# Routing the first four tiles of a mixture of experts ahead of the other twelve, in an eight-block transformer kernel on one Trainium2 core

## Chip, cores and metric

The kernel runs on one core of a Trainium2 chip. The metric is the device time of one execution in microseconds (us); less is better. Engines: PE (matrix products), DVE (VectorE), ACT (ScalarE), POOL (GpSimd), SP (which issues the loads).

## The reference

The input is x of shape (2, 1024, 128), fp32: 2048 tokens, D = 128. Eight residual blocks follow each other, each on the layer-normed x: a window attention, a mixture of experts, a causal attention, the same mixture again, a cope attention, a six-layer local stack, a linear attention, and the local stack again. The change touches the mixture:

```python
logits = xt @ gate_w.T                      # (2048, 8)
scores = softmax(logits); top_vals, idx = top_k(scores, 2)
xs = xt[:, None, :] * weights[:, :, None]   # weights: the scores of the chosen
for e in range(8):
    mask = (idx == e)
    h  = silu(xs @ w1[e].T + b1[e])         # 128 -> 128
    x2 = h @ w2[e].T + b2[e]
    x3 = xs @ w3[e].T + b3[e]
    y  = y + sum(x2 * x3 * mask)
z = silu(xt @ sw1.T) * (xt @ sw2.T) @ sw3.T # shared expert, 256 wide
x = x + y + z
```

## The kernel before

X (2048 tokens as NT = 16 tiles of 128 tokens on the partitions) stays in SBUF through all blocks. A block is a stage: each engine has its own program, written out by hand in the order in which it is to run (`pe`, `act`, `dve`, `pool`), and waits on semaphores for the others; a barrier (`fence`) ends the stage. `mixture` is run twice, with the tags `f_` and `g_`, on the same weights, which were loaded long before; no DMA is issued in it.

All eight experts are computed for every token, with the score as scale and a 0/1 mask of the two best. In the beginning the 16 tiles are normed in four groups of four: DVE measures (lines 202 to 209), POOL takes the power (213), DVE applies (222), PE transposes (238), ACT copies the result to XNT (245), PE multiplies the four tiles by the gate (603). Then DVE copies the four groups' gate outputs (716) and does the softmax for all 16 tiles at once (656 to 664), with ACT's Exp between (621). PE waits at line 605 for the copies of all groups before its first large product.

The loop over the tiles follows. For tile i:
- PE `up(i)` (572, 576): eight w1, eight w3 and the shared expert's products, banks 0 to 4 of PSUM; the last waits for `zadd_out`.
- DVE `up(i)` (689) scales w1's products by the score and adds b1; ACT does Silu on them (633); PE turns them (563), ACT copies (628), PE `down(i)` (584).
- ACT does Silu of the shared half (637), DVE multiplies by the other half (`gated`, 695), PE turns it (590), ACT copies (649), PE `shared_down` (596), DVE adds to X (722).
- ACT scales w3's products to x3 (644). POOL adds b3 (738) and multiplies by the mask (740).
- DVE `down(i)` adds b2 (703) and multiplies by x3 (707). POOL adds the eight experts in three steps (745), and to X (748).

The order on DVE is: z add of tile i-1, `up(i)`, `gated(i)`, at i = 0 `choose()`, `down(i-1)`. The order on POOL is: b3 and mask of tile i, then the tree of tile i-1; after tile 15 one more tree ends the stage. `choose()` (671 to 681) makes the mask for all 16 tiles with five instructions of 1024 elements and one of 128: two comparisons of each score with each other, a product with a table that settles ties, a sum, a reduction, and "fewer than 1.5 rivals". At tile 0 ACT waits for that mask before it scales x3 (line 641).

Of the kernel before, what the change touches and what calls it, by code (L numbers as in the profile page):

```python
# [9 lines left out]
ALU = mybir.AluOpType  # L10
# [43 lines left out]
def build(nc, t, out):  # L54
    ctx = ExitStack()
    with ctx:
# [477 lines left out]
        def mixture(tag):  # L534
            with ExitStack() as own:
# [12 lines left out]

                def xt(i):
                    return XNT[:, A_WIN + i * P:A_WIN + (i + 1) * P]

                def pe():
# [41 lines left out]
                            m = te.matmul(PS[:, 4, I_SH:I_SH + D], sT[:, j * P:(j + 1) * P], sw3[:, j, :], start=(j == 0), stop=(j == 1))  # L596
                        m.then_inc(z_mm)

                    for g in range(NG):
                        norm_turn(g, xn4[:, g % 2, :, :])  # L600
                        te.wait_ge(xT_out, g + 1)
                        for j in range(4):
                            m = te.matmul(PS[:, 1 + g, j * E_N:(j + 1) * E_N], xt(4 * g + j), gate[:, :], start=True, stop=True)
                        m.then_inc(gate_mm)
                    te.wait_ge(gate_out, NG)
                    for i in range(NT + 1):
                        if i:
                            turn(i - 1)
                            shared_down(i - 1)
                        if i < NT:  # L610
                            up(i)
                        if i:
                            down(i - 1)
                        if i < NT:
                            shared_turn(i)

                def act():
                    for g in range(NG):
                        norm_copy(g, kept_T(g))
                    ac.wait_ge(scores_out, 1)  # L620
                    ac.activation(sc[:, :, :], sc[:, :, :], ACT.Exp).then_inc(sc_exp)
                    for i in range(NT + 1):
                        if i:
                            for n, bank in ((0, 6), (1, 5)):
                                ac.wait_ge(h_turn, 2 * (i - 1) + n + 1)
                                if i >= 2:
                                    ac.wait_ge(y_mm, 2 * (i - 2) + n + 1)
                                ac.copy(hT[:, 4 * n:4 * n + 4, :].rearrange("p a b -> p (a b)"), PS[:, bank, :]).then_inc(hT_out)
                        if i < NT:
                            for n in range(2):  # L630
                                h = hin[:, i % 2, 4 * n:4 * n + 4, :]
                                ac.wait_ge(hin_out, 2 * i + n + 1)
                                ac.activation(h, h, ACT.Silu).then_inc(silu_out)
# [12 lines left out]
                            ac.wait_ge(sg_turn, i + 1)  # L646
                            if i >= 1:
                                ac.wait_ge(z_mm, i)
                            ac.copy(sT[:, :], PS[:, 4, 0:I_SH]).then_inc(sT_out)

                def dve():
                    all3, four = [P, NT, E_N], [P, NT, E_N, E_N]

                    def scores():
                        V.wait()
                        V.step(ve.tensor_reduce(r1[:, :], sc[:, :, :], AX, ALU.max))
                        V.wait()
                        ve.tensor_tensor(sc[:, :, :], sc[:, :, :], over(r1[:, :], 2, all3), ALU.subtract).then_inc(scores_out)
                        ve.wait_ge(sc_exp, 1)
                        V.step(ve.tensor_reduce(r1[:, :], sc[:, :, :], AX, ALU.add))  # L660
                        V.wait()
                        V.step(ve.reciprocal(r1[:, :], r1[:, :]))
                        V.wait()
                        V.step(ve.tensor_tensor(sc[:, :, :], sc[:, :, :], over(r1[:, :], 2, all3), ALU.mult))
                        V.wait()

                    def choose():
                        gt4 = gt[:, :, :].rearrange("p t (a b) -> p t a b", a=E_N)
                        eq4 = eq[:, :, :].rearrange("p t (a b) -> p t a b", a=E_N)
                        rival, own_s = over(sc[:, :, :], 2, four), over(sc[:, :, :], 3, four)  # L670
# [3 lines left out]
                        V.step(ve.tensor_tensor(eq[:, :, :], eq[:, :, :],  # L674
                                                over(lower[:, :, :].rearrange("p a b -> p (a b)"), 1, [P, NT, E_N * E_N]), ALU.mult))
                        V.wait()
                        V.step(ve.tensor_tensor(gt[:, :, :], gt[:, :, :], eq[:, :, :], ALU.add))
                        V.wait()
                        V.step(ve.tensor_reduce(mask[:, :, :], gt4, AX, ALU.add))
                        V.wait()  # L680
                        ve.tensor_scalar(mask[:, :, :], mask[:, :, :], 1.5, None, ALU.is_lt).then_inc(mask_out)

                    def up(i):
                        if i >= 2:
# [24 lines left out]
                    norm_stats(0, X)  # L709
                    for g in range(NG):  # L710
                        if g < NG - 1:
                            norm_stats(g + 1, X)
                        norm_apply(g, X, xn4[:, g % 2, :, :])
                    for g in range(NG):
                        ve.wait_ge(gate_mm, g + 1)
                        ve.tensor_copy(sc[:, 4 * g:4 * g + 4, :], PS[:, 1 + g, 0:4 * E_N].rearrange("p (j e) -> p j e", j=4)).then_inc(gate_out)
                    ve.wait_ge(gate_out, NG)
                    scores()
                    for i in range(NT + 1):
                        if i:  # L720
                            ve.wait_ge(z_mm, i)
                            ve.tensor_tensor(X[:, i - 1, :], PS[:, 4, I_SH:I_SH + D], X[:, i - 1, :], ALU.add).then_inc(zadd_out)
                        if i < NT:
                            up(i)
                            gated(i)
                        if i == 0:
                            choose()
                        if i:
                            down(i - 1)

                def pool():
                    for g in range(NG):
                        norm_root(g)
                    for i in range(NT + 1):
                        if i < NT:
                            x = x3[:, i % 2, :, :]
                            gp.wait_ge(x3_out, 2 * i + 2)
                            G.step(gp.tensor_tensor(x, x, b3[:, :, :], ALU.add))
                            G.wait()
                            gp.tensor_tensor(x, x, over(mask[:, i, :], 2, [P, E_N, D]), ALU.mult).then_inc(x3m_out)  # L740
                        if i:
# [1284 lines left out]
```

## Time and profile before

| | |
|---|---|
| median of 3 runs | 4230.68 us (4227.46 to 4234.22) |
| profiled execution | 4232.35 us, span 4230.3 us, mean granted TensorE clock 0.947 |
| PE busy | 3803.1 us, 90% of the span |
| DVE busy | 3017.7 us, 71% |
| POOL busy | 2675.5 us, 63% |
| ACT busy | 2586.9 us, 61% |
| first mixture, first norm to the next stage's first norm | 169.78 to 343.36 us |
| second mixture, the same | 415.74 to 589.19 us |

The profile is one execution. Times in it are counted from the span's start; "busy" leaves out waits. The two mixtures together are 347 us of 4230, the two local stacks some 3,200. Matrix products in fp32 are done in several passes, so a product of the code shows as more than one instruction. "idle before <- releaser" says how long the engine stood still before an instruction and what released it. The duration of a DVE or POOL instruction includes time in which it is issued but held up.

### The profile page before, as it was taken

The numbers are of one execution on the slowest core, as the hardware profiler recorded it, in microseconds if no ns is written. First come the engines' busy times: TensorE is split into PE (matmuls) and PEld (weight loads), VectorE is DVE, ScalarE is ACT, GpSimd is POOL, SyncE is SP. The second block draws the span as 40 slices with busy tenths as digits, with TensorE's granted clock in tenths as the row PEclk, the third lists the DMA queues.
The fourth block names the chain that finished last, engine by engine and source line by source line (L and its number), as shares of the span: only waits on it lengthen the run. The fifth ranks groups of instructions, "written<-read, shape, count | busy, mean of one in ns | idle before, by whom it ended". The sixth has DMA issues, their size and how long they took to land. (4 is left out here: it accounts for less than half of the span.)

```text
span 4230.3 us, 158783 instructions
## 1 busy us (share of the span) xinstructions
PE 3803.1 (90%) x66896; PEld 2661.8 (63%) x66896; DVE 3017.7 (71%) x6190; ACT 2586.9 (61%) x4965; POOL 2675.5 (63%) x2263
## 2 busy tenths in 40 slices
PE   7896863999999999999999568999999999999996
PEld 5564542666766666666666435676666666676664
DVE  6675657777777777877778257777877777777773
ACT  4463531667666676766676325666667676766764
POOL 2192663776767676767667237776767667676762
PEclk9898885999999999999999759999999999999998
DMA  3000000333333333333233102333333233332222
GB/s 100 1 1 1 1 1 0 98 79 79 83 75 89 82 80 80 80 80 91 65 94 80 34 0 70 85 77 91 78 80 95 66 92 79 78 90 71 70 65 56
DMA packets 303234, 276.83 MB, mean 65 GB/s; under 512 B 158136, under 2 KB 201664, under 8 KB 302528
## 3 DMA queue, kind: packets, MB, share of 16 engines
q1 hardware_dynamic: 302528, 266.68, 24.8%
q8 instruction: 533, 8.73, 0.9%
q14 instruction: 173, 1.42, 0.1%
HBM read 51.58 MB, written 1.05 MB: 12 GB/s over the span
## 5 line engine op out<-in xcount | busy, mean ns | idle before, releaser
L1433 PE MATMUL PS<-l_wqkv,XNT 128*128 128x512 f32 x768 | 386.0, 625 | 0.6 <-issue 0.5
L1427 PE MATMUL PS<-l_wqkv,XNT 128*128 128x512 f32 x768 | 381.1, 618 | 2.2 <-issue 1.1
L1420 PE MATMUL PS<-l_wqkv,XNT 128*128 128x512 f32 x768 | 366.7, 600 | 6.4 <-DVE l_UQ L1702 2.7
L1575 ACT ACTIVATE m_sq<-PS 128x512 f32<-128x512 f32 x384 | 226.1, 596 | 198.8 <-PE PS L1427 162.0
L1575 ACT ACTIVATE l_sq<-PS 128x512 f32<-128x512 f32 x384 | 226.2, 596 | 194.6 <-PE PS L1427 159.9
L1841 POOL TENSOR_TENSOR l_Pm<-l_Pm,l_rs 128x1024 f32<-128x1024 f32 x96 | 182.8, 1905 | 237.6 <-DVE l_rs L1712 237.6
L1841 POOL TENSOR_TENSOR m_Pm<-m_Pm,m_rs 128x1024 f32<-128x1024 f32 x96 | 182.8, 1904 | 235.8 <-DVE m_rs L1712 235.8
L1699 DVE TENSOR_TENSOR m_QR<-PS,l_rot 128x512 f32<-128x512 f32 x192 | 131.8, 687 | 165.2 <-ACT m_sq L1575 159.0
L1699 DVE TENSOR_TENSOR l_QR<-PS,l_rot 128x512 f32<-128x512 f32 x192 | 131.8, 687 | 163.4 <-ACT l_sq L1575 157.2
L1730 DVE TENSOR_TENSOR XN<-PS,XN 128x128 f32<-128x128 f32 x192 | 56.2, 293 | 269.3 <-PE PS L1479 269.3
L1836 POOL TENSOR_TENSOR m_QR<-m_QR,m_UQ 128x1024 f32<-128x1024 f32 x96 | 227.8, 2373 | 19.3 <-DVE m_UQ L1702 19.3
L1836 POOL TENSOR_TENSOR l_QR<-l_QR,l_UQ 128x1024 f32<-128x1024 f32 x96 | 227.7, 2372 | 19.0 <-DVE l_UQ L1702 19.0
L1836 POOL TENSOR_TENSOR l_KR<-l_KR,l_UK 128x1024 f32<-128x1024 f32 x96 | 226.9, 2363 | 0.2 <-DVE l_UK L1702 0.2
L1836 POOL TENSOR_TENSOR m_KR<-m_KR,m_UK 128x1024 f32<-128x1024 f32 x96 | 226.8, 2363 | 0.2 <-DVE m_UK L1702 0.2
L1717 DVE TENSOR_REDUCE m_sums<-m_sq 128x16 f32<-128x1024 f32 x192 | 219.1, 1183 | 0.0
L1717 DVE TENSOR_REDUCE l_sums<-l_sq 128x16 f32<-128x1024 f32 x192 | 219.1, 1183 | 0.0
L1449 PEld LDWEIGHTS PS<-l_V,l_pT 64*32 64x32 f32 x12288 | 132.7, 106 | 127.3 <-issue 69.9
L1449 PEld LDWEIGHTS PS<-m_V,m_pT 64*32 64x32 f32 x12288 | 131.2, 105 | 118.8 <-issue 81.3
L1433 PEld LDWEIGHTS PS<-l_wqkv,XNT 128*128 128x128 f32 x768 | 132.4, 192 | 114.0 <-issue 96.8
L1427 PEld LDWEIGHTS PS<-l_wqkv,XNT 128*128 128x128 f32 x768 | 130.7, 189 | 115.4 <-issue 95.9
L1449 PE MATMUL PS<-l_V,l_pT 64*32 64x64 f32 x12288 | 155.5, 228 | 48.0 <-DMA l_V<-l_Vt 31.5
L1420 PEld LDWEIGHTS PS<-l_wqkv,XNT 128*128 128x128 f32 x768 | 132.5, 193 | 102.2 <-issue 102.2
(373 smaller groups left out, 11170.7 us busy)
## 6 DMA issues: line engine op xcount, KB each, us to landing
l_V<-l_Vt SPq DMA_DIRECT2D x576, 128.0 KB
m_V<-m_Vt SPq DMA_DIRECT2D x576, 128.0 KB
l_V<-l_Vt SPq DMA_DIRECT2D x384, 64.0 KB
m_V<-m_Vt SPq DMA_DIRECT2D x384, 64.0 KB
l_wqkv<-l_wqkv_dram SPq DMA_DIRECT2D x144, 128.0 KB, 2.4
l_rot<-l_rot_dram SPq DMA_DIRECT2D x48, 256.0 KB, 3.9
l_wo<-l_wo_dram SPq DMA_DIRECT2D x24, 256.0 KB, 3.7
l_w<-l_w_dram SPq DMA_DIRECT2D x12, 341.0 KB
```

The source lines that it names most:

```text
L1420: te.matmul(PS[:, b, :], tile_T(n), weights(n, b * 512, (b + 1) * 512), start=True, stop=True).then_inc(q_pr)
L1427: te.matmul(PS[:, 2 + b, :], tile_T(n), weights(n, INNER + b * 512, INNER + (b + 1) * 512), start=True, stop=True).then_inc(k_pr)
L1433: m = te.matmul(PS[:, r, :], tile_T(n), wv, start=True, stop=True)
L1449: m = te.matmul(PS[LW * w:LW * (w + 1), 6 + r, c * LD:(c + 1) * LD], pT[64 * r:64 * r + 64, c, LW * w:LW * (w + 1)], V2[64 * r:64 * r + 64 ...
L1575: ac.activation(sq[:, c, b * 512:(b + 1) * 512], PS[:, 2 * c + b, :], ACT.Square).then_inc(sq_out)
L1699: ve.tensor_tensor(R[:, n % 2, heads, :], src, over(rot[:, par, 2 * c, i, :], 1, [P, 8, LD]), ALU.mult)
L1717: ve.tensor_reduce(sums2[:, c * LH:(c + 1) * LH, 0], sq[:, c, :].rearrange("p (h d) -> p h d", d=LD), AX, ALU.add).then_inc(ssr_out)
L1730: ve.tensor_tensor(Y[:, i, :], PS[:, 5, 0:D], Y[:, i, :], ALU.add).then_inc(y_add)
L1836: gp.tensor_tensor(R[:, n % 2, :, :], R[:, n % 2, :, :], U[:, :, :], ALU.add).then_inc((aq_out, ak_out)[c])
L1841: gp.tensor_tensor(pm, pm, over(rs[:, :], 2, [P, 16, 2 * LW]), ALU.mult).then_inc(pn_out)
```

## The change

The first group (tiles 0 to 3) is gated, its softmax done, and tile 0's products made, before the other groups are transposed and gated. The softmax of tiles 4 to 15 is done at i = 1 on DVE, its Exp on ACT behind tile 0; their masks are made in three slices of four tiles at i = 2, 3 and 4. ACT no longer waits for the mask; POOL does, before the mask's product of tiles 0, 4, 8 and 12. All gate outputs share PSUM bank 5, and the transposes alternate between banks 6 and 7. The tree of tile 15 and its add to X are moved from POOL to DVE.

```diff
+                FIRST, OTHERS = slice(0, 4), slice(4, NT)
...
-                    for g in range(NG):
-                        norm_turn(g, xn4[:, g % 2, :, :])
...
+                    def gates(g):
                         te.wait_ge(xT_out, g + 1)
...
+                        if g == 1:
+                            te.wait_ge(gate_out, 1)
+                        for i in range(4 * g, 4 * g + 4):
+                            m = te.matmul(PS[:, 5, i * E_N:(i + 1) * E_N], xt(i), gate[:, :], start=True, stop=True)
                         m.then_inc(gate_mm)
-                    te.wait_ge(gate_out, NG)
+
+                    rows_turn(0)
+                    gates(0)
+                    rows_turn(1)
+                    up(0)
+                    for g in range(2, NG):
+                        rows_turn(g)
+                        gates(g - 1)
+                    gates(NG - 1)
+                    te.wait_ge(gate_out, 2)
+                    te.wait_ge(xT_out, NG)
                     for i in range(NT + 1):
                         if i:
                             turn(i - 1)
                             shared_down(i - 1)
-                        if i < NT:
+                        if 0 < i < NT:
                             up(i)
...
                 def act():
...
+                    rows_copy(0)
+                    rows_copy(1)
+                    exponent(0, FIRST)
+                    rows_copy(2)
+                    rows_copy(3)
                     for i in range(NT + 1):
...
-                            if i == 0:
-                                ac.wait_ge(mask_out, 1)
...
+                        if i == 0:
+                            exponent(1, OTHERS)
...
                 def dve():
...
+                    def choose(tiles):
+                        n = tiles.stop - tiles.start
+                        four = [P, n, E_N, E_N]
+                        g_t, e_t, s_t = gt[:, tiles, :], eq[:, tiles, :], sc[:, tiles, :]
...
                         ve.tensor_tensor(gt4, rival, own_s, ALU.is_gt)
                         V.step(ve.tensor_tensor(eq4, rival, own_s, ALU.is_equal))
                         V.wait()
...
+                        V.step(ve.tensor_tensor(e_t, e_t, over(lower[:, :, :].rearrange("p a b -> p (a b)"), 1, [P, n, E_N * E_N]), ALU.mult))
                         V.wait()
...
+                        V.step(ve.tensor_tensor(g_t, g_t, e_t, ALU.add))
                         V.wait()
...
+                        V.step(ve.tensor_reduce(mask[:, tiles, :], gt4, AX, ALU.add))
                         V.wait()
...
+                        ve.tensor_scalar(mask[:, tiles, :], mask[:, tiles, :], 1.5, None, ALU.is_lt).then_inc(mask_out)
...
                         ve.tensor_tensor(y, y, x3[:, i % 2, :, :], ALU.mult).then_inc(y3_out)
...
+                        if i == NT - 1:
+                            ve.wait_ge(y3_out, NT)
+                            for n in (4, 2, 1):
+                                V.step(ve.tensor_tensor(y[:, 0:n, :], y[:, 0:n, :], y[:, n:2 * n, :], ALU.add))
+                                V.wait()
+                            ve.wait_ge(zadd_out, NT)
+                            V.step(ve.tensor_tensor(X[:, i, :], X[:, i, :], y[:, 0, :], ALU.add))
...
+                    stats(0)
+                    stats(1)
+                    apply(0)
+                    stats(2)
+                    apply(1)
+                    stats(3)
+                    ve.wait_ge(gate_mm, 1)
+                    take_gates(FIRST)
+                    shifted_scores(0, FIRST)
+                    apply(2)
+                    scores(0, FIRST)
+                    apply(3)
+                    up(0)
+                    gated(0)
+                    choose(FIRST)
+                    ve.wait_ge(gate_mm, NG)
+                    take_gates(OTHERS)
+                    shifted_scores(1, OTHERS)
+                    for i in range(1, NT + 1):
+                        ve.wait_ge(z_mm, i)
+                        ve.tensor_tensor(X[:, i - 1, :], PS[:, 4, I_SH:I_SH + D], X[:, i - 1, :], ALU.add).then_inc(zadd_out)
                         if i < NT:
                             up(i)
                             gated(i)
...
+                        down(i - 1)
+                        if i == 1:
+                            scores(1, OTHERS)
+                        if 2 <= i < 5:
+                            choose(slice(4 * i - 4, 4 * i))
 
                 def pool():
...
+                            if i % 4 == 0:
+                                gp.wait_ge(mask_out, 1 + i // 4)
                             gp.tensor_tensor(x, x, over(mask[:, i, :], 2, [P, E_N, D]), ALU.mult).then_inc(x3m_out)
-                        if i:
+                        if 0 < i < NT:
                             y = y8[:, (i - 1) % 2, :, :]
```

`rows_turn(g)` and `rows_copy(g)` are the norm's transposes and copies with the new banks; `take_gates`, `shifted_scores` and `scores` hold the instructions of lines 716 and 656 to 664 for a part of the tiles; `exponent` holds line 621.

## Rows read from the trace of the kernel before

**Rows 1.** Stage windows, tiles 1 to 15: length, busy us and instructions per engine, clock, DMA

```profile
206.00:331.00 125.00, 120.04 (x616) 80.00 (x614) 88.29 (x196) 75.52 (x210) 114.43 (x87) 0.99 0.00 1
```

**Rows 2.** Timeline, POOL: start, us, engine, line, operation, idle before and releaser

```profile
213.64 2.36 POOL L738 TENSOR_TENSOR f_x<-f_x,f_b 128x1024 f32<-128x1024 f32 x1 [5.61 <-ACT f_x L644]
216.08 2.76 POOL L740 TENSOR_TENSOR f_x<-f_x,f_mask 128x1024 f32<-128x1024 f32 x1
...
222.43 3.05 POOL L738 TENSOR_TENSOR f_x<-f_x,f_b 128x1024 f32<-128x1024 f32 x1 [0.49 <-ACT f_x L644]
225.55 1.90 POOL L740 TENSOR_TENSOR f_x<-f_x,f_mask 128x1024 f32<-128x1024 f32 x1
...
230.10 0.46 POOL L748 TENSOR_TENSOR X<-X,f_y 128x128 f32<-128x128 f32 x1
...
330.80 2.35 POOL L738 TENSOR_TENSOR f_x<-f_x,f_b 128x1024 f32<-128x1024 f32 x1
...
339.02 2.59 POOL L745 TENSOR_TENSOR f_y<-f_y 128x512 f32<-128x512 f32 x3
341.69 0.45 POOL L748 TENSOR_TENSOR X<-X,f_y 128x128 f32<-128x128 f32 x1
```

**Rows 3.** Timeline ahead of tile 0's x3, PE and ACT

```profile
177.26 1.09 PE L238 MATMUL PS<-ident,xn 128*128 128x128 f32 x4
...
188.19 5.19 PE L572 MATMUL PS<-f_w,XNT 128*128 128x512 f32 x8 [0.28 <-DVE f_sc L716]
...
189.14 1.28 ACT L633 ACT_TABLE_LOAD   x1
...
201.45 2.18 ACT L644 ACTIVATE f_x<-PS,f_sc 128x128 f32<-128x128 f32 x8 [6.79 <-DVE f_mask L681]
```

**Rows 4.** Timeline of tiles 1 to 3 and of the end, DVE, ACT and PE

```profile
213.69 3.39 DVE L707 TENSOR_TENSOR f_y<-f_y,f_x 128x1024 f32<-128x1024 f32 x1
...
217.21 2.14 DVE L689 SCALAR_TENSOR_TENSOR f_hin<-PS,f_sc,f_b 128x128 f32<-128x128 f32 x8
...
219.38 0.63 ACT L633 ACTIVATE f_hin<-f_hin 128x512 f32<-128x512 f32 x1 [0.40 <-DVE f_hin L689]
...
222.04 1.23 DVE L707 TENSOR_TENSOR f_y<-f_y,f_x 128x1024 f32<-128x1024 f32 x1
...
223.21 3.60 PE L572 MATMUL PS<-f_w,XNT 128*128 128x512 f32 x8
...
335.16 2.27 DVE L707 TENSOR_TENSOR f_y<-f_y,f_x 128x1024 f32<-128x1024 f32 x1 [2.99 <-POOL f_x L740]
```

**Rows 5.** DVE groups: one line's min/median/max ns; one group's busy us and mean ns

```profile
L1215 DVE TENSOR_TENSOR d_den<-d_dots x4: 224/224/1236, 2442.3 to 2501.6; 128x64 f32<-128x64 f32 x4
...
L995 DVE TENSOR_TENSOR c_gates<-c_gates 128x256 f32<-128x256 f32 x1 | 0.4, 424 | 0.0
```

**Rows 6.** Windows of one us, PE: length, busy us and instructions, granted clock, DMA

```profile
203.00:204.00 1.00, 0.06 (x1) 0.50 0.00 0
...
208.00:209.00 1.00, 1.00 (x3) 0.85 0.00 0
```

**Rows 7.** Timeline, ACT in the local stack: a table load and what follows

```profile
2013.88 1.28 ACT L1672 ACT_TABLE_LOAD   x1
2015.17 1.19 ACT L1575 ACTIVATE l_sq<-PS 128x512 f32<-128x512 f32 x2
```

**Rows 8.** Timeline, DVE and POOL in the linear attention

```profile
2500.20 1.26 POOL L1294 TENSOR_TENSOR d_an<-d_an,d_gain 128x512 f32<-128x512 f32 x1 [1.96 <-ACT d_an L1193]
2501.04 0.57 DVE L1214 TENSOR_TENSOR d_dots<-d_dots,d_turn 128x128 f32<-128x128 f32 x1
2501.54 1.26 POOL L1296 TENSOR_TENSOR d_an<-d_an,d_gain 128x512 f32<-128x512 f32 x1
2501.64 1.24 DVE L1215 TENSOR_TENSOR d_den<-d_dots 128x64 f32<-128x64 f32 x1
...
2502.92 1.27 DVE L1216 TENSOR_SCALAR d_den<-d_den 128x64 f32<-128x64 f32 x1
```

More of the change, by code:

```diff
@@ L597, in shared_down, with rows_turn @@
                         m.then_inc(z_mm)
-                    for g in range(NG):
-                        norm_turn(g, xn4[:, g % 2, :, :])
+                    def rows_turn(g):
+                        te.wait_ge(xn_out, g + 1)
+                        if g >= 2:
+                            te.wait_ge(xT_out, g - 1)
+                        for j in range(4):
+                            m = te.transpose(PS[:, 6 + g % 2, j * P:(j + 1) * P], xn4[:, g % 2, j, :], ident[:, :])
+                        m.then_inc(turn_mm)
+                    def gates(g):
                         te.wait_ge(xT_out, g + 1)
-                        for j in range(4):
-                            m = te.matmul(PS[:, 1 + g, j * E_N:(j + 1) * E_N], xt(4 * g + j), gate[:, :], start=True, stop=True)
+                        if g == 1:
+                            te.wait_ge(gate_out, 1)
+                        for i in range(4 * g, 4 * g + 4):
+                            m = te.matmul(PS[:, 5, i * E_N:(i + 1) * E_N], xt(i), gate[:, :], start=True, stop=True)
                         m.then_inc(gate_mm)
-                    te.wait_ge(gate_out, NG)
+                    rows_turn(0)
[8 more added lines that the diff above has]
+                    te.wait_ge(xT_out, NG)
                     for i in range(NT + 1):
@@ L617, in act, with rows_copy, exponent @@
                 def act():
[L618 to L621, printed above, removed]
+                    def rows_copy(g):
+                        ac.wait_ge(turn_mm, g + 1)
+                        ac.copy(kept_T(g), PS[:, 6 + g % 2, :]).then_inc(xT_out)
+                    def exponent(part, tiles):
+                        ac.wait_ge(scores_out, part + 1)
+                        ac.activation(sc[:, tiles, :], sc[:, tiles, :], ACT.Exp).then_inc(sc_exp)
+                    rows_copy(0)
[3 more added lines that the diff above has]
+                    rows_copy(3)
                     for i in range(NT + 1):
@@ L649, in act, with take_gates @@
                             ac.copy(sT[:, :], PS[:, 4, 0:I_SH]).then_inc(sT_out)
+                        if i == 0:
+                            exponent(1, OTHERS)
                 def dve():
-                    all3, four = [P, NT, E_N], [P, NT, E_N, E_N]
-                    def scores():
-                        V.wait()
-                        V.step(ve.tensor_reduce(r1[:, :], sc[:, :, :], AX, ALU.max))
+                    def take_gates(tiles):
+                        ve.tensor_copy(sc[:, tiles, :], PS[:, 5, tiles.start * E_N:tiles.stop * E_N].rearrange("p (t e) -> p t e", e=E_N)).then_inc(gate_out)
@@ new lines, in shifted_scores, with scores @@
+                    def shifted_scores(part, tiles):
+                        n = tiles.stop - tiles.start
+                        ve.wait_ge(gate_out, part + 1)
+                        V.step(ve.tensor_reduce(r1[:, tiles], sc[:, tiles, :], AX, ALU.max))
+                        V.wait()
+                        ve.tensor_tensor(sc[:, tiles, :], sc[:, tiles, :], over(r1[:, tiles], 2, [P, n, E_N]), ALU.subtract).then_inc(scores_out)
+                    def scores(part, tiles):
+                        n = tiles.stop - tiles.start
+                        ve.wait_ge(sc_exp, part + 1)
+                        V.step(ve.tensor_reduce(r1[:, tiles], sc[:, tiles, :], AX, ALU.add))
@@ L657, in scores @@
                         V.wait()
-                        ve.tensor_tensor(sc[:, :, :], sc[:, :, :], over(r1[:, :], 2, all3), ALU.subtract).then_inc(scores_out)
-                        ve.wait_ge(sc_exp, 1)
-                        V.step(ve.tensor_reduce(r1[:, :], sc[:, :, :], AX, ALU.add))
+                        V.step(ve.reciprocal(r1[:, tiles], r1[:, tiles]))
                         V.wait()
-                        V.step(ve.reciprocal(r1[:, :], r1[:, :]))
+                        V.step(ve.tensor_tensor(sc[:, tiles, :], sc[:, tiles, :], over(r1[:, tiles], 2, [P, n, E_N]), ALU.mult))
@@ L663, in scores @@
                         V.wait()
[L664 to L670, printed above, removed]
+                    def choose(tiles):
+                        n = tiles.stop - tiles.start
+                        four = [P, n, E_N, E_N]
+                        g_t, e_t, s_t = gt[:, tiles, :], eq[:, tiles, :], sc[:, tiles, :]
+                        gt4, eq4 = (a.rearrange("p t (a b) -> p t a b", a=E_N) for a in (g_t, e_t))
+                        rival, own_s = over(s_t, 2, four), over(s_t, 3, four)
@@ L673, in choose @@
                         V.wait()
-                        V.step(ve.tensor_tensor(eq[:, :, :], eq[:, :, :],
-                                                over(lower[:, :, :].rearrange("p a b -> p (a b)"), 1, [P, NT, E_N * E_N]), ALU.mult))
+                        V.step(ve.tensor_tensor(e_t, e_t, over(lower[:, :, :].rearrange("p a b -> p (a b)"), 1, [P, n, E_N * E_N]), ALU.mult))
                         V.wait()
-                        V.step(ve.tensor_tensor(gt[:, :, :], gt[:, :, :], eq[:, :, :], ALU.add))
+                        V.step(ve.tensor_tensor(g_t, g_t, e_t, ALU.add))
                         V.wait()
-                        V.step(ve.tensor_reduce(mask[:, :, :], gt4, AX, ALU.add))
+                        V.step(ve.tensor_reduce(mask[:, tiles, :], gt4, AX, ALU.add))
                         V.wait()
-                        ve.tensor_scalar(mask[:, :, :], mask[:, :, :], 1.5, None, ALU.is_lt).then_inc(mask_out)
+                        ve.tensor_scalar(mask[:, tiles, :], mask[:, tiles, :], 1.5, None, ALU.is_lt).then_inc(mask_out)
                     def up(i):
@@ L707, in down @@
                         ve.tensor_tensor(y, y, x3[:, i % 2, :, :], ALU.mult).then_inc(y3_out)
[L709 to L712, printed above, removed]
-                        norm_apply(g, X, xn4[:, g % 2, :, :])
-                    for g in range(NG):
-                        ve.wait_ge(gate_mm, g + 1)
-                        ve.tensor_copy(sc[:, 4 * g:4 * g + 4, :], PS[:, 1 + g, 0:4 * E_N].rearrange("p (j e) -> p j e", j=4)).then_inc(gate_out)
@@ L717, in dve @@
-                    ve.wait_ge(gate_out, NG)
-                    scores()
-                    for i in range(NT + 1):
-                        if i:
-                            ve.wait_ge(z_mm, i)
-                            ve.tensor_tensor(X[:, i - 1, :], PS[:, 4, I_SH:I_SH + D], X[:, i - 1, :], ALU.add).then_inc(zadd_out)
+                        if i == NT - 1:
[5 more added lines that the diff above has]
+                            V.step(ve.tensor_tensor(X[:, i, :], X[:, i, :], y[:, 0, :], ALU.add))
@@ new lines, in stats, with apply @@
+                    def stats(g):
+                        norm_stats(g, X)
+                    def apply(g):
+                        norm_apply(g, X, xn4[:, g % 2, :, :])
+                    stats(0)
[8 more added lines that the diff above has]
+                    apply(2)
@@ L725, in dve @@
                             gated(i)
[L726 to L729, printed above, removed]
+                        down(i - 1)
[3 more added lines that the diff above has]
+                            choose(slice(4 * i - 4, 4 * i))
                 def pool():
@@ L739, in pool @@
                             G.wait()
+                            if i % 4 == 0:
+                                gp.wait_ge(mask_out, 1 + i // 4)
                             gp.tensor_tensor(x, x, over(mask[:, i, :], 2, [P, E_N, D]), ALU.mult).then_inc(x3m_out)
-                        if i:
+                        if 0 < i < NT:
                             y = y8[:, (i - 1) % 2, :, :]
```

## The prediction

> **What bounds the kernel now.** I read the stretch of a mixture by windows first, because the change touches nothing else (it issues and moves no DMA, and SP's queue has no part in it): in the 125 us between tile 1's gating and the last tile, PE is busy 120.04 us, POOL 114.43 and DVE 88.29 [rows 1]. So two engines are nearly full and DVE looks free for a third of the time. Then POOL's timeline [rows 2]: its first bias add of a tile (line 738) for tile 1 starts at 213.64 us after 5.61 us of idleness, for tile 2 at 222.43 after 0.49, and the one of tile 15 at 330.80 with no idleness noted: 117.16 us for 14 tiles, 8.37 each. From tile 3 on POOL never waits; it has six instructions per tile (3.05, really 2.35 when nothing blocks it, then 1.90, three adds and 0.45; the last five run from 225.55 to 230.56). The stage ends with POOL's own last sum at 342.14. Before the loop the reader should see how long everything waits for routing [rows 3]: PE ends the second group's transposes at 178.35, but starts the big matmuls at 188.19, and ACT can scale x3 of tile 0 only at 201.45, after 6.79 us of waiting for the mask. The second mixture, read the same way, repeats all this to a few hundredths, so I work one out and double it.
>
> **What the start gains.** `up(0)` on PE needs only group 0's transposed rows, and in its new place it begins at 178.35 instead of 188.19, 9.8 us sooner. What then stands before POOL's tile 1? `up(0)` costs 5.19 for eight passes and some 0.9 for the last two, partly at the low clock [rows 3]: it ends near 183.8. ACT now has both remaining copies of rows queued ahead of tile 0's Silu, and they wait for PE: two sets of transposes (about 0.6 each at the full clock, 1.09 at the low one) and one set of gates (eight short passes, about 1 by estimate) stand behind `up(0)`, then a copy of 0.6: 186.6. Then the Silu table, 1.28 [rows 3], which was hidden before and no longer is, since the compiler puts it right ahead of the first Silu: 187.9. Two Silus, the shared Silu and x3 take 3.6 (from 219.38 to 222.43 is 3.05, plus one more Silu start of 0.5 [rows 4]): POOL gets tile 0 at about 191.5. DVE meanwhile gates at 189.8 and then chooses for four tiles: five instructions of 256 elements at 0.42 [rows 5] and a short one, 2.4 us with gaps instead of 6.4. Its last one is due at about 192.0 and probably lands behind POOL's 2.35; then it ends at 194.1. PE waits for the copy of the other gates behind that choice, so it resumes at 194.4, at the low clock (in 203 to 204 us, where it had 0.06 us of work, the granted clock was 0.50, and it was 0.85 only in 208 to 209, four us after the work came back [rows 6]): ten transposes of 0.27, shared_down 1.2 and ten passes of 0.43 to 0.44 (eight take 3.60 [rows 4]) end at 202.7, and x3 plus gaps 2.5 later: 205.2 against 213.64, that is -8.4. If the last short instruction is not caught, -9.9. I take **-9.0**.
>
> **Two more table loads.** The second Exp stands between two Silus, so ACT loads three tables where it loaded one. A load takes 1.28 us and the next instruction starts 0.01 us behind it (2013.88 plus 1.28 is 2015.16, next at 2015.17 [rows 7]). From 195.4 on ACT has load, Exp, two copies, load: ready at about 199.7, before tile 1's first Silu is due at about 200.5. Cover: PE's slow restart. Without it, it would cost up to 2.6. I count 0.
> The Trainium skill ("ScalarE: Activation LUTs", What ACT_TABLE_LOAD costs) gives about 2.66 us for every switch, a 1.38 us drain with the load, and asks to batch activations by set, which speaks against this change. The trace shows no such drain beside its load. By the page the sum would be some 2.3 us per mixture, 5 in all, higher.
>
> **What the other groups' choice costs.** This is the term that decides. The diff puts the softmax of tiles 4 to 15 at i=1 and a choice for four tiles at i=2, 3 and 4, each time on DVE behind `down`, in a place where POOL has just been given x3 and is busy for 7.5 us. Alone, a slice costs the 2.4 us above. But look at what a DVE instruction that reads two tensors from SBUF does beside POOL: line 707 takes 1.23 alone and 3.39 or 2.27 when a POOL instruction is running [rows 4]. In the linear attention the same is seen in a chain of small ones [rows 8]: line 1214 takes 0.57, and ends when POOL's 1.26 us instruction does; POOL's next starts, and line 1215 takes 1.24 (alone 0.22, [rows 5]); and then line 1216, a tensor_scalar, 1.27. So the two take turns by whole instructions, also across a semaphore gap. A slice has four two-input instructions and one tensor_scalar; each waits for one POOL instruction, so that DVE gets out only when POOL has finished all its six: from the start of line 738 that is 7.5 (POOL) + 1.2 (line 707) + 1.3 to 1.4 (what of the slice is not under POOL's) or about 10. From DVE's freedom to the next x3 at POOL is 5.4: z add 0.2, then 217.21 to 222.43 [rows 4]. One tile with a slice so lasts about **15.4** instead of 8.37. PE, queued behind zadd_out and sg_out, stalls 5 us in each and falls to the low clock, which I leave within the 15.4. The softmax at i=1 has one two-input instruction with POOL's 1.90 to 2.76 in front of it and two small reads: **+2.3**, between 0.7 and 2.8.
> After tile 5 all goes on at 8.37; neither engine can win anything back, since POOL is full and PE has 120.04 of 125 us filled [rows 1]. Tile 1 to 15: (8.79 + 2.3) + 3 x 15.4 + 10 x 8.37 = 141.0 against 117.16, **+23.8**. Bounds for a slice: 2.4 less 1.3 of slack at each tile (+1.1) if DVE never waits, +8 if PE's slow clock also delays `down`.
>
> **The end.** POOL no longer does the last tree (339.02 to 342.14 [rows 2]); DVE does it from 337.43, where its product ends [rows 4]. Its three adds and the add to X (the one of 256 elements 0.42 [rows 5], the others around it, some 1.7 in all) again take turns with what POOL still has of tile 14's tree until 339.0, and end near 340.7: **-1.5**, between 0 and -3.1.
>
> The sum: -9.0 + 23.8 - 1.5 = +13.3 per mixture, +26.6 for both. The profiled execution has 4232.35 (span 4230.3 and 2.05 around it), which is 1.67 above the median 4230.68: I predict **4257**.
>
> **Rivals.**
> A: DVE passes POOL freely, as its instructions that read PSUM do (line 689, eight in 2.14 at 217.21 [rows 4], beside POOL's 216.08 to 218.84 [rows 2]). For it: the slices' instructions are small; against it: line 707 [rows 4] and the small ones of [rows 8]. Then -9.9 + 0.7 + 3 x 1.1 - 3.1 = -9.0 per mixture, 4213: **faster**. It decides as long as a slice holds the next tile up by less than about 2 us. Chance 0.13.
> B: DVE waits once per slice and then keeps its turn through the chain: 2.35 + 2.4 - 1.3 = +3.5 a slice: -9.5 + 2.3 + 10.5 - 1.5 = +1.8 per mixture, 4234: no change that can be told. For it: the two comparisons of a slice have no semaphore between them; against it: in [rows 8] three links of a chain in a row each waited anew. Chance 0.13.
> C: the start does not gain, because the copies of groups 2 and 3, queued ahead of the Silu, hold ACT longer than I count. Every us there is one at the end; with POOL's tile 1 at 209 instead of 204.6 the result is 4266. It is on my own side, and within the range.
> D: the change does nothing, POOL being full anyway: excluded for the start, since POOL is idle until 213.64 but for one tile.
>
> **Numbers.** Forecast (C with it) 0.74, own range 4241 to 4270; A 0.13; B 0.13. A measurement of this kernel tells 0.2%, 8.5 us, from no change. Range 4230 to 4270: it leaves out A, the lower part of B and 0.04 above. Faster 0.13, same 0.13, slower 0.74.
>
> **What would show it.** In the profile after: line 738 of tile 1 near 204 to 205; tiles 2 to 5 some 15 us apart, with POOL idle for 5 us or more before each and the choice's 256-element instructions at 0.7 to 2.4 us instead of 0.42; then 8.3 again; three table loads, with no gap of ACT behind them; granted clock under 1 in tiles 3 to 5. If the slices run at 0.42 each, A holds and I am wrong on the sign. If only the first is long, B.

## The result, and the profile after

| | before | after |
|---|---|---|
| median | 4231.81 us | 4240.89 us |
| profiled execution | 4232.35 us, span 4230.3 | 4238.61 us, span 4237.2 |
| ratio after / before | | 1.0024, 95% interval [1.0015, 1.0032] |

Both medians are of twelve executions; one of those before and two of those after ran 2% longer at a lower granted clock, and the ratio leaves them out. The change makes the kernel slower by a quarter of a per cent, some 10 us. The direction was forecast; the size was not: 4257 stands for 26 us, 2.6 times as much.

POOL's timeline of the first mixture after the change (start, us, engine, line, operation, idle before and what ended it) is the counterpart of [rows 2]; line 796 is the old 738, 800 is 740, 805 is 745, 808 is 748:

```profile
191.30 2.34 POOL L796 TENSOR_TENSOR f_x<-f_x,f_b 128x1024 f32<-128x1024 f32 x1 [12.65 <-ACT f_x L673]
193.83 1.90 POOL L800 TENSOR_TENSOR f_x<-f_x,f_mask 128x1024 f32<-128x1024 f32 x1 [0.19 <-DVE f_mask L718]
204.58 2.35 POOL L796 TENSOR_TENSOR f_x<-f_x,f_b 128x1024 f32<-128x1024 f32 x1 [8.85 <-ACT f_x L673]
...
215.36 3.05 POOL L796 TENSOR_TENSOR f_x<-f_x,f_b 128x1024 f32<-128x1024 f32 x1 [2.47 <-ACT f_x L673]
218.48 1.96 POOL L800 TENSOR_TENSOR f_x<-f_x,f_mask 128x1024 f32<-128x1024 f32 x1
220.40 2.89 POOL L805 TENSOR_TENSOR f_y<-f_y 128x512 f32<-128x512 f32 x3
223.37 0.45 POOL L808 TENSOR_TENSOR X<-X,f_y 128x128 f32<-128x128 f32 x1
229.21 2.36 POOL L796 TENSOR_TENSOR f_x<-f_x,f_b 128x1024 f32<-128x1024 f32 x1 [5.38 <-ACT f_x L673]
...
243.56 2.36 POOL L796 TENSOR_TENSOR f_x<-f_x,f_b 128x1024 f32<-128x1024 f32 x1 [5.70 <-ACT f_x L673]
...
258.05 2.35 POOL L796 TENSOR_TENSOR f_x<-f_x,f_b 128x1024 f32<-128x1024 f32 x1 [5.85 <-ACT f_x L673]
...
342.19 2.34 POOL L796 TENSOR_TENSOR f_x<-f_x,f_b 128x1024 f32<-128x1024 f32 x1
```

Tile 1 comes at 204.58 instead of 213.64: that is the gain of the start. Then the tiles with a slice come 13.85, 14.35 and 14.49 us apart, with POOL idle for 5.4 to 5.9 us before each, where the mean before was 8.37. From tile 5 to tile 15 it is 84.14 us, 8.4 each, and tile 15 is 11.4 us later than before.

What DVE did between the first two of those tiles (its timeline, the first slice; 709 to 718 are the old 671 to 681, 744 is 707):

```profile
214.97 1.23 DVE L744 TENSOR_TENSOR f_y<-f_y,f_x 128x1024 f32<-128x1024 f32 x1
216.11 2.57 DVE L709 TENSOR_TENSOR f_gt<-f_sc 128x256 f32<-128x256 f32 x1
218.61 2.11 DVE L710 TENSOR_TENSOR f_eq<-f_sc 128x256 f32<-128x256 f32 x1
220.76 1.37 DVE L712 TENSOR_TENSOR f_eq<-f_eq,f_lower 128x256 f32<-128x256 f32 x1
222.16 0.83 DVE L714 TENSOR_TENSOR f_gt<-f_gt,f_eq 128x256 f32<-128x256 f32 x1
223.02 0.42 DVE L716 TENSOR_REDUCE f_mask<-f_gt 128x32 f32<-128x256 f32 x1
223.47 0.39 DVE L718 TENSOR_SCALAR f_mask<-f_mask 128x32 f32<-128x32 f32 x1
```

Read beside POOL's rows above: line 709 ends 0.3 us behind POOL's 796 (215.36 plus 3.05 is 218.41), 710 ends 0.3 behind 800, and so on, one POOL instruction for each. The same 256 elements take 0.42 us where POOL stands still. Only the reduction, with one input, keeps its 0.42. This slice takes 7.8 us instead of 2.4, the other two 5.6 each, with line 744 held up ahead of them (2.50 and 3.15 us instead of 1.23).

PE stood still meanwhile, and its granted clock fell, as forecast: it was 0.50 from 224 to 228 us. But from the slice's last instruction on DVE to POOL's next bias add it is 5.35, 5.35 and 5.49 us; in the kernel before, at the full clock, it was 5.35 from line 707 to the bias add (217.08 to 222.43 [rows 4, rows 2]). So the slower PE adds at most 0.1 us here.

The end of the stage, on DVE and POOL:

```profile
346.54 2.27 DVE L744 TENSOR_TENSOR f_y<-f_y,f_x 128x1024 f32<-128x1024 f32 x1 [2.99 <-POOL f_x L800]
348.84 2.15 DVE L748 TENSOR_TENSOR f_y<-f_y 128x512 f32<-128x512 f32 x3
350.32 0.52 POOL L808 TENSOR_TENSOR X<-X,f_y 128x128 f32<-128x128 f32 x1
351.02 0.29 DVE L751 TENSOR_TENSOR X<-X,f_y 128x128 f32<-128x128 f32 x1
352.50 0.87 DVE L202 BATCH_NORM_STATS2 stats<-X 128x6 f32<-128x128 f32 x4 [1.18 <-PEq L121]
```

From tile 15's bias add to the next stage's first norm it is 10.31 us, before 12.56.

So each mixture is 9 us longer, 18 in sum, but the span is only 6.9 longer. To find the rest I measured every stage from its first norm (line 202, released by the barrier) to the next one's; the linear attention has no such line and is taken from its first memset. In us, in this order: mixture, causal, mixture, cope, local stack, linear, local stack, and the sum of the five that are not mixtures:

```
          mixture  causal  mixture    cope    local  linear    local      sum
before    173.58   72.38  173.45  109.07  1714.48  110.42  1707.14   3713.5
after     182.71   70.05  182.41  107.16  1707.96  106.72  1710.40   3702.3
```

The five other stages, whose code the change does not touch, are 11.2 us shorter. This is what the forecast left out. The windows over causal, cope and the first local stack (length, then busy us and instructions of PE, PE's weight loads, DVE, ACT and POOL, then granted clock and DMA), before and after in turn:

```profile
343.36:415.74 72.38, 56.55 (x320) 41.46 (x320) 38.23 (x137) 28.36 (x65) 4.18 (x4) 0.90 0.00 1
352.50:422.55 70.05, 54.21 (x320) 39.85 (x320) 38.23 (x136) 28.37 (x65) 4.17 (x4) 0.93 0.00 1
```

```profile
589.19:698.26 109.07, 36.33 (x96) 22.74 (x96) 63.71 (x104) 7.28 (x12) 20.96 (x37) 0.56 0.00 0
604.96:712.12 107.16, 34.57 (x96) 22.11 (x96) 63.56 (x103) 7.27 (x12) 20.96 (x37) 0.56 0.00 0
```

```profile
698.26:2412.74 1714.48, 1608.56 (x31584) 1135.29 (x31584) 1265.45 (x2528) 1135.30 (x2112) 1160.29 (x984) 0.98 0.31 78
712.12:2420.10 1707.98, 1607.41 (x31584) 1135.09 (x31584) 1265.66 (x2528) 1134.63 (x2112) 1160.01 (x985) 0.98 0.31 79
```

In causal and cope PE is busy 2.3 and 1.8 us less for the same instructions, and that is what the stages lost (2.3 and 1.9). In the first local stack PE is busy only 1.2 us less, and the stage is 6.5 shorter.

### The profile page after: what moved, and what is told of

Read it like the earlier page. It is cut to its first block and busy times, and to the rows that moved or that the text cites. A ratio compares the mean times of both kernels' runs of the same rounds, so it can differ in the third digit from the quotient of the medians.

```text
span 4237.2 us, 158843 instructions
## 1 busy us (share of the span) xinstructions
PE 3797.5 (90%) x66896; PEld 2660.4 (63%) x66896; DVE 3060.7 (72%) x6240; ACT 2591.0 (61%) x4971; POOL 2671.6 (63%) x2255
## 5 line engine op out<-in xcount | busy, mean ns | idle before, releaser
L1509 PE MATMUL PS<-m_V,m_pT 64*32 64x64 f32 x12288 | 153.9, 226 | 43.6 <-DMA m_V<-m_Vt 26.3
```

Source lines behind the costliest of these rows:

```text
L1509: m = te.matmul(PS[LW * w:LW * (w + 1), 6 + r, c * LD:(c + 1) * LD], pT[64 * r:64 * r + 64, c, LW * w:LW * (w + 1)], V2[64 * r:64 * r + 64 ...
```

## The experiments

**Both kernels once more, unchanged** (`r_before`, `r_after`).

> The kernel before once more, for its stage lengths. Theory 'the other stages vary from run to run': causal, cope, linear and the two local stacks differ from the first profile (72.4, 109.1, 110.5, 1714.5 and 1707.1 us) by several us in sum, either way, while the two mixtures stay at 173.6 and 173.5. Rival 'the other stages depend only on the kernel': they repeat within 1 us in sum.

> The changed kernel once more. In its first profile the mixtures were 182.7 and 182.4 us long, 18.1 more than before in sum, and all other stages together 11.1 less. Theory 'vary from run to run': the mixtures repeat, the other stages' sum moves by several us. Rival 'the change shortens the others by a fixed amount': the sum of the others is again some 11 us below that of the kernel before.

```
r_before  173.47   72.33  173.38  109.09  1714.54  110.43  1707.61   3714.0
r_after   182.63   70.00  182.44  107.10  1708.57  116.43  1704.59   3706.7
```

Neither theory in full. Causal, cope and the first local stack repeat within 0.6 us in both kernels. But the linear attention took 116.43 in one run of the changed kernel and 106.72 in the other, though it began only 0.2 us later, and the last local stack took 5.8 less. The windows over the stage (columns as above), the first from the changed kernel's first profile, the second from its repeat:

```profile
2420.10:2526.80 106.70, 64.79 (x208) 39.02 (x208) 50.77 (x146) 25.74 (x57) 32.92 (x28) 0.60 0.00 0
```

```profile
2420.30:2536.70 116.40, 74.55 (x208) 44.22 (x208) 50.76 (x145) 25.72 (x57) 32.92 (x28) 0.51 0.00 0
```

The same instructions, and DVE, ACT and POOL as busy as before; PE is 10 us busier at a lower granted clock. In four of these microseconds (PE alone) PE had the full clock in one run and half of it in the other:

```profile
2492.10:2496.10 4.00, 2.65 (x14) 1.00 0.00 0
```

```profile
2492.30:2496.30 4.00, 3.31 (x13) 0.50 0.00 0
```

The causal attention shows it too: before, the clock came back at 358 us, 11 us after PE's first work at 347.3; after, at 362, 5.5 us after it (356.5). The place in the span does not decide it alone: in `r_before` the seven stages begin 1.0 to 1.3 us earlier than in the first profile, and none of them differs by more than 0.5 us.

**Padding in place of the change** (`e_pad`, `e_pad3`). The kernel before, with idle work at the end of each mixture:

```diff
+                    ve.wait_ge(tree_out, NT)
+                    for n in range(7):        # e_pad3: range(3)
+                        V.step(ve.tensor_tensor(gt[:, :, :], gt[:, :, :], eq[:, :, :], ALU.add))
+                        V.wait()
```

> The kernel before, with seven idle DVE instructions of 1.26 us at the end of each mixture: both get 8.9 us longer, as in the changed kernel, and everything else keeps its code. Theory P (where a stage begins decides when TensorE's clock comes back and how the later stages run): causal takes about 70.0 us instead of 72.4, cope 107.1 instead of 109.1, the first local stack 1708 instead of 1714.5, the others 7 to 11 us less in sum, and the total rises by 7 to 11 us (1.0017 to 1.0026), not by 17.8. Rival (the changed kernel's other order or addresses make the others shorter): they stay at 3713.5 in sum, and the total rises by 17.8 us (1.0042).

> The same with three instructions, 3.8 us per mixture. Theory P: stage lengths differ again from those of before, by up to some us either way, and repeat none of the two patterns exactly; the total need not rise by 7.6 us. Rival: the others stay at 3713.5 and the total rises by 7.6 us (1.0018).

```
e_pad     182.34   70.12  182.42  107.22  1708.11  106.71  1710.94   3703.1
```

Every one of the five stages is within 0.6 us of the changed kernel's first profile, with none of its code. The ratio is 1.0027, [1.0016, 1.0039], for 17.7 us (0.42%) of added time, and cannot be told from the change's 1.0024. So the missing 11 us do not come from the changed code: they come with the later beginning of the stages behind it. In causal, cope and linear attention (7.9 us of it) PE is busy less and the granted clock is seen to differ: in causal it came back 9.5 us behind the first norm after the change and 9.7 in `e_pad`, 15.1 before; in linear it was 0.60 on the mean in both, 0.56 before; in the two local stacks (6.5 less and 3.3 more) the clock is 0.98 either way and the cause is not shown. With three instructions the ratio was 1.0018, [1.0009, 1.0028]. That is what was added, 7.6 us by estimate from `e_pad`'s instructions, but the interval also allows some us less: it does not settle whether a smaller shift is given back in part. That kernel's stage lengths were not compared.

**POOL held off during a slice** (`e_hold`), the changed kernel with one more wait:

```diff
                             gp.wait_ge(x3_out, 2 * i + 2)
+                            if 2 <= i < 5:
+                                gp.wait_ge(mask_out, i)
```

> POOL waits for the slice's mask before it adds b3 at tiles 2, 3 and 4, so DVE chooses without taking turns with POOL. Theory (turns by whole instructions cost the time): a slice takes 2.4 us instead of 7.7, the tiles with one come 10 us apart instead of 14.2, the stage ends some 9 us sooner per mixture, total 18 below the changed kernel and 9 below the kernel before (0.998), though a wait was added. Rival (the DVE work itself, or ACT's table loads, or PE's clock cost it): the added wait makes it the same or slower than the changed kernel, 1.002 or more against before.

0.9974, [0.9961, 0.9987] of the kernel before; mixtures 169.44 and 169.40 us, 13 less than in the changed kernel, where 9 were expected. On DVE and POOL, the first slice and what follows:

```profile
214.39 0.42 DVE L709 TENSOR_TENSOR f_gt<-f_sc 128x256 f32<-128x256 f32 x1
214.72 0.42 DVE L710 TENSOR_TENSOR f_eq<-f_sc 128x256 f32<-128x256 f32 x1
...
216.55 0.18 DVE L718 TENSOR_SCALAR f_mask<-f_mask 128x32 f32<-128x32 f32 x1
...
216.87 2.36 POOL L798 TENSOR_TENSOR f_x<-f_x,f_b 128x1024 f32<-128x1024 f32 x1 [5.71 <-DVE f_mask L718]
```

The same work in 2.3 us (3.3 in the other two slices, which begin beside POOL's tree), and tiles 2 to 5 come at 216.87, 226.84, 236.81 and 245.07: 9.97, 9.97 and 8.26 us apart, no longer 14. A wait was added and 13 us per mixture went away. The rivals "the work itself" and "table loads" fall, since both are still there. PE kept the full clock here (1.00 from 198 to 240 us); that its fall in the changed kernel was a consequence is read from the 5.35 us above.

**Turns without work** (`e_tiny`, `e_tinyr`). The kernel before, with five tiny instructions behind `down` at i=2, 3 and 4; `e_tinyr` has `tensor_reduce(r1[:, 0:1], r1[:, 0:4], AX, ALU.max)` in their place:

```diff
+                        if 2 <= i < 5:
+                            for n in range(5):
+                                V.step(ve.tensor_tensor(r1[:, 0:4], r1[:, 0:4], r1[:, 4:8], ALU.add))
+                                V.wait()
```

> The kernel before, with five chained two-input additions of 4 elements on DVE behind down at i=2, 3 and 4, on data that nobody uses: 0.16 us of work each, 0.8 us per tile. Theory (what a slice costs is DVE's turns with POOL, not its work): each waits for a POOL instruction of 0.45 to 2.4 us, the chain takes 5 to 7 us, tiles 3 to 5 come 12 to 13.5 us apart at POOL instead of 8.6 on average, and each mixture gets 12 us or more longer (185 to 190 us). Rival (the slices' own DVE work delays the tiles): 0.8 us is less than the slack, the mixtures stay within 1 us of 173.5.

> The same with five reductions of 4 elements, which read one tensor. Theory: they do not wait for POOL, 0.16 to 0.2 us each, and the mixtures stay within 1 us of 173.5 us. If they too wait, it is not the second input that matters.

Groups of the two lines (min/median/max ns, first and last start):

```profile
L732 DVE TENSOR_TENSOR f_r<-f_r x15: 161/1182/2312, 223.6 to 254.0; 128x4 f32<-128x4 f32 x15
```

```profile
L732 DVE TENSOR_REDUCE f_r<-f_r x15: 145/157/159, 224.0 to 241.0; 128x1 f32<-128x4 f32 x15
```

Additions of four elements: 0.16 us at best, 1.18 in the median, 2.31 at most; the first chain of five is one row of 5.70 us. POOL's tiles 2 to 5 came at 222.88, 234.81, 246.74 and 259.64, 12.3 us apart, and the mixtures were 185.7 and 186.0 us long. For 0.8 us of work per tile that is more than the whole change cost a mixture. The total was 4242.54 us against 4228.18 before, one execution of each. The reductions never waited (4228.95 in all), and from tile 1 to tile 6 that kernel took 42.76 us, exactly as before (213.64 to 256.40). Its mixtures were still 2.1 and 2.4 us longer than before, which the expectation of 1 us missed. In the first, all of it lies ahead of tile 1, where no instruction was added: PE's eight passes for tile 0 took 6.62 us instead of 5.19 and those for tile 1 5.97 instead of 5.26, since the full clock came back 5.9 us behind the first of them instead of 3.0 (192.8 and 191.2 us), and at tile 1 at 209.9 instead of 208.2. I had not expected that within the mixtures. The Trainium skill ("SBUF — State Buffer", the section on who interferes with whom) states that a VectorE instruction with two inputs in SBUF contends with a GpSimd instruction that reads SBUF, and that a reduction on this chip never contends: 1.18 us against 0.157 agrees.

**The end alone** (`e_tail`): the kernel before with the change's last seven lines of DVE's `down` and POOL's `0 < i < NT`.

> The kernel before with only the end of the change: the tree of tile 15 and its add to X by VectorE. Theory: each mixture 2.2 us shorter (171.3 instead of 173.5), as tile 15 to the next stage took 10.3 instead of 12.6 us in the changed kernel. Rival (its gain there came from the late tiles' lag): under 1 us per mixture. Of the total nothing can be told from no change under theory P, as the other stages move by more.

Mixtures 171.46 and 171.81 us, 2.1 and 1.6 less. The ratio is 0.9987, [0.9977, 0.9997].

**The choice in POOL's gap** (`e_gap`): the changed kernel, with the other groups' softmax and choice ahead of the loop, where POOL is idle from 195.7 to 204.6 us:

```diff
                     shifted_scores(1, OTHERS)
+                    scores(1, OTHERS)
+                    choose(OTHERS)
                     for i in range(1, NT + 1):
...
-                        if i == 1:
-                            scores(1, OTHERS)
-                        if 2 <= i < 5:
-                            choose(slice(4 * i - 4, 4 * i))
...
-                                gp.wait_ge(mask_out, 1 + i // 4)
+                                gp.wait_ge(mask_out, min(2, 1 + i // 4))
```

> Softmax and choice of all twelve other tiles at once on DVE behind the shifted scores at tile 0, while POOL is idle between its tile 0 and tile 1. Theory: five instructions of 768 elements at 0.96 us, 5 us in all and undisturbed; POOL's tile 1 comes at 208 instead of 204.6 us, but tiles 2 to 5 then follow 8.4 us apart; with the end by VectorE each mixture is 7 to 8 us shorter than before, total 15 below before (0.9964). Rival (what costs the time in tiles 2 to 5 is not the choice beside POOL): tiles 2 to 5 keep more than 10 us each, and the total stays above 0.998.

```profile
196.57 0.96 DVE L709 TENSOR_TENSOR f_gt<-f_sc 128x768 f32<-128x768 f32 x1
...
201.41 0.21 DVE L718 TENSOR_SCALAR f_mask<-f_mask 128x96 f32<-128x96 f32 x1
```

Three slices' work in 5.1 us. Tile 1 comes at 206.96, the next three 8.10, 9.29 and 8.25 us apart. Mixtures 164.92 and 165.05, total 0.9967, [0.9955, 0.998] of the kernel before: faster than the kernels before and after the change.

**A version that goes further** (`e_best`): as `e_gap`, but the other groups' scores, shifted scores and Exp come ahead of tile 0's Silu, `choose(OTHERS)` stands behind `gated(0)`, and POOL starts tile 0 only when all masks are there:

```diff
                     rows_copy(3)
+                    exponent(1, OTHERS)
                     for i in range(NT + 1):
...
-                        if i == 0:
-                            exponent(1, OTHERS)
...
-                    gated(0)
-                    choose(FIRST)
                     ve.wait_ge(gate_mm, NG)
                     take_gates(OTHERS)
                     shifted_scores(1, OTHERS)
+                    choose(FIRST)
                     scores(1, OTHERS)
+                    gated(0)
                     choose(OTHERS)
...
                             gp.wait_ge(x3_out, 2 * i + 2)
+                            if i == 0:
+                                gp.wait_ge(mask_out, 2)
...
-                            if i % 4 == 0:
-                                gp.wait_ge(mask_out, 1 + i // 4)
```

> As e_gap, with the other groups' scores and their Exp ahead of tile 0's Silu (one table load in place of three), their choice behind gated(0), and POOL held off tile 0 until it is done. Theory (DVE's turns with POOL, 2 us twice, delay PE's restart): POOL's tile 1 comes at 202.6 us (from a start of 169.0) instead of 207.0, mixtures 160.6 us instead of 165.0, total 0.994 to 0.996 of before. Rival (ACT's Silu, later by Exp and the wait for the others' scores, is what PE waits for): tile 1 no earlier than 206, mixtures 165.

```profile
191.64 0.42 DVE L731 TENSOR_TENSOR f_sg<-f_sg,PS 128x256 f32<-128x256 f32 x1 [0.18 <-ACT f_sg L669]
...
197.16 2.36 POOL L795 TENSOR_TENSOR f_x<-f_x,f_b 128x1024 f32<-128x1024 f32 x1 [18.36 <-DVE f_mask L717]
...
203.71 2.36 POOL L795 TENSOR_TENSOR f_x<-f_x,f_b 128x1024 f32<-128x1024 f32 x1 [2.21 <-ACT f_x L674]
```

Counted from the stage's first norm (169.94 here, 169.00 there), POOL begins tile 0 six us later than in `e_gap` and tile 1 four us sooner. Mixtures 161.24 and 160.04, total 0.993, [0.9918, 0.9942], median 4201.13 against 4229.13 of the kernel before: the fastest version of this study. It changes several things at once (DVE's turns with POOL, one table load for three); what each is worth was not tried apart.

## Why the prediction was right about the mixture and wrong about the total

- **The start** was forecast as -9.0 and was -9.06 (204.58 against 213.64). The last short instruction of the first choice was caught behind POOL, as feared: 1.99 us instead of 0.18, until 193.7. PE resumed at 193.90 (forecast 194.4). Two of its sums are off by a little and moved nothing: 178.35 with 5.19 and 0.9 is 184.4, not 183.8 (`up(0)` ended at 184.08), and with the last instruction not caught its terms give -10.5, not -9.9.
- **The two more table loads** cost nothing, as counted. Of the three, the one ahead of tile 0's Silu stood in the open and was in the sum; behind the other two ACT still waited 0.92 us for DVE (ACT's timeline):

```profile
195.02 1.28 ACT L646 ACT_TABLE_LOAD   x1
196.31 0.28 ACT L646 ACTIVATE f_sc<-f_sc 128x96 f32<-128x96 f32 x1
196.50 1.06 ACT L659 COPY f_hT<-PS 128x512 f32<-128x512 f32 x2
197.57 1.28 ACT L664 ACT_TABLE_LOAD   x1
199.78 0.63 ACT L664 ACTIVATE f_hin<-f_hin 128x512 f32<-128x512 f32 x1 [0.92 <-DVE f_hin L726]
```

  The next instruction came 0.01 us behind a load of 1.28. The Trainium skill ("ScalarE: Activation LUTs", the section on what a table load costs) adds a drain of 1.38 us to each switch; it is not in these rows. With it, the prediction's own terms (two drains less 0.8 us of cover, and one in the open) would give 3.3 us a mixture, an estimate, and not its 2.3.
- **The softmax at i=1** was +2.3: tile 1 to 2 is 10.78 against 8.79, +2.0.
- **The slices** were the first wrong size. "One tile with a slice so lasts about 15.4" was 14.2 on the mean. The 5.4 in it was right; the 10, from POOL's bias add to the slice's last instruction, was 8.5, 9.0 and 9.0. By the rows of the second slice all three of its terms were too large: POOL's own work is 7.3 us, not 7.5; line 744 held POOL up for 0.9, not 1.2 (line 800 took 2.76 instead of 1.90); and what of the slice is not under POOL's came to some 0.7, not 1.35, since its instructions end 0.3 us behind POOL's and not the full 0.42. That is 3.5 us per mixture too much. The mechanism, and rival A's and B's defeat, stand by the rows, `e_hold`, `e_tiny` and `e_tinyr`.
- **The end** was forecast as -1.5 and was -2.25 here; alone it gave 1.6 to 2.1.
- **The sum** for a mixture was +13.3 and was +9.1 and +9.0. This alone would have given a total near 4249: of the 26.6 us forecast, 8.5 are lost here, 7 to 11 in the next step.
- **The step that failed** is the one from the mixtures to the total: "+26.6 for both", on the profiled execution, as if all else stayed. The five other stages gave back 11.2 us in the first profile and 7 in the repeat. Padding with no part of the change did the same (10.4). The mixture's rows held a hint: I used the late return of the clock [rows 6] inside the mixture and never asked what a shift does to causal, cope and linear attention, where the granted clock is 0.90, 0.56 and 0.56 on the mean.
- Rival B, "4234: no change", came nearest in time, by luck: DVE waited anew at each link of the chain, which B denies. C did not occur: both copies were done at 186.4, as counted.

What stays open: why the first local stack, at a granted clock of 0.98 in both kernels, takes 1714.5 us in one and 1708.0 in the other. The padding shows that it needs no changed code; which of its waits does it was not tried. Nor is it known what in the beginning of a stage sets its length. The same sum of the five stages, which no experiment edits, was 3698.5 us in `e_hold`, 3699.4 in `e_tiny`, 3703.5 in `e_gap`, 3706.0 in `e_best`, 3706.3 in `e_tinyr` and 3716.0 in `e_tail`, against 3713.5 and 3714.0 in the two profiles of the kernel before. So part of every total here is theirs: `e_hold`'s profiled execution is 24.5 us shorter than that of the kernel before, of which its mixtures account for 8.2. What each experiment says of the mixture is read from the mixture's length.

## What to carry to other kernels

Work put "in the shadow" of a full engine is in no shadow if the two engines hold each other up: before moving a chain of small two-input VectorE instructions beside a busy GpSimd, count one GpSimd instruction per link, not its elements; put the chain where GpSimd is idle, or hold GpSimd for it. And where stages run at a half clock for part of their time, a change that moves their beginning by some us can itself move the total by some 0.2%. So compare stage by stage, and pad the old kernel by the same time before believing a small difference in the total.

## What the runs showed of the hardware that was not expected

- An added wait made a kernel faster by 13 us per mixture (`e_hold`).
- Fifteen additions of four elements lengthened a mixture by 12.2 us (185.73 against 173.58, `e_tiny`).
- The linear attention took one of three lengths, 106.7, 110.4 or 116.4 us, in all eleven profiles in which it was read, with a granted clock of 0.60, 0.56 or 0.51; the changed kernel had the first and the last, with 0.2 us between the beginnings.
- A lone tensor_scalar of 32 elements waited for POOL like a two-input instruction (1.99 us instead of 0.18); a reduction did not (0.157 us in the median, `e_tinyr`). Not every tensor_scalar beside a POOL instruction does: four of line 222 took 1.11 us at 172.58, beside POOL's line 213 (four elements, 172.75 to 173.79), and 1.12 at 179.91 without it.
